# Products of three field pairs from whole tables instead of from the batch's rows, in a pairwise-product recommendation kernel

## What is computed

```python
e = jnp.stack([tbl_0[ids[:, 0]], ..., tbl_39[ids[:, 39]]], axis=1)   # (2048, 40, 64)
viW = jnp.einsum('bpd,pde->bpe', e[:, i_idx, :], W)                  # 780 pairs
z = jnp.einsum('bpe,bpe->bp', viW, e[:, j_idx, :])
h = jnp.concatenate([z, dense_ctx], axis=1)
h = jnp.maximum(h @ W_top1 + b_top1, 0.0)
h = jnp.maximum(h @ W_top2 + b_top2, 0.0)
y = h @ W_top3
```

## Time and profile before

| | us |
|---|---|
| median of 3 runs | 1150.31 (1150.08 to 1150.65) |
| the profiled execution | 1150.38 |
| its span, first to last instruction | 1148.6 |
| PE busy | 1123.7 (98%) |
| DVE busy | 979.0 (85%) |
| ACT busy | 907.7 (79%) |
| POOL busy | 695.8 (61%) |

### The profile page before, as it was taken

The page is one execution under the profiler, slowest core; times in us unless marked ns, Lnnn a source line. Parts: engine busy times, 40 slices in busy tenths (PEclk is TensorE's granted clock), DMA queues, the critical chain, the costliest instruction groups (busy, mean ns, idle before and its releaser), DMA issues.

```text
span 1148.6 us, 46937 instructions
## 1 busy us (share of the span) xinstructions
PE 1123.7 (98%) x17728; PEld 443.4 (39%) x17728; DVE 979.0 (85%) x901; ACT 907.7 (79%) x7245; POOL 695.8 (61%) x837
## 2 busy tenths in 40 slices
PE   6989999999999999999999999999999999999998
PEld 2333333333445333333345433333344533333345
DVE  8599999999866889999975779999986688999960
ACT  1489999998466889999765779999946688999961
POOL 6766655555667667777667767767666766632110
PEclk9999999999999999999999999999999999999999
DMA  6233353232522332333432323333252233222210
GB/s 175 45 95 90 87 152 86 74 92 68 142 54 60 76 88 69 99 89 72 110 103 45 87 71 73 91 89 75 68 144 55 54 82 80 72 80 73 59 32 1
DMA packets 79248, 93.47 MB, mean 81 GB/s; under 512 B 19248, under 2 KB 63040, under 8 KB 78892
## 3 DMA queue, kind: packets, MB, share of 16 engines
q1 hardware_dynamic: 58920, 69.48, 21.2%
q0 software_dynamic: 19456, 19.96, 9.6%
q10 hardware_dynamic: 648, 1.03, 0.3%
HBM read 79.91 MB, written 0.01 MB: 70 GB/s over the span
## 4 chain that ended last, share of the span: by engine, by line
PE 76%; ACT 12%; DVE 7%; issue 4%; DMA 0%; SPq 0%; DVEq 0%
PE Ups L911 29%; PE Ups L904 15%; PE Zps L927 15%; ACT PB L701 11%; PE Ups L956 7%; DVE P L831 4%; PE Ups L889 3%; PE Ups L874 3%; PE Ups L969 3%; DVE PB L819 2%; PE Ups L962 1%; DVE zB L787 1%; DMA V<-tbl 0%; PE Ups L944 0%; ACT V L709 0%
## 5 line engine op out<-in xcount | busy, mean ns | idle before, releaser
L701 ACT ACTIVATE PB<-PB 128x64 f32<-128x64 f32 x3588 | 858.2, 242 | 61.6 <-DVE PB L819 59.4
L701 ACT ACTIVATION_READ_ACCUMULATOR PB<-PB 128x1 f32 x3588 | 674.8, 188 | 0.0
L678 POOL DMA_INDIRECT stage<-tbl,idx x512 | 485.5, 948 | 270.6 <-PE Ups L911 81.9
L831 DVE TENSOR_TENSOR P<-Ups,V 128x1024 f32<-128x1024 f32 x492 | 585.1, 1217 | 45.8 <-PE Ups L911 43.0
L911 PE MATMUL Ups<-V,wf 64*32 64x512 f32 x8192 | 519.1, 591 | 6.8 <-ACT V L709 2.3
L819 DVE TENSOR_TENSOR PB<-Ups,VN 128x1024 f32<-128x1024 f32 (+1 forms) x272 | 327.2, 1203 | 33.6 <-PE Ups L904 30.8
L904 PE MATMUL Ups<-wf,V 64*32 64x512 f32 (+1 forms) x4352 | 287.9, 585 | 4.2 <-DVE P L831 2.4
L927 PE MATMUL Zps<-P,sel 64*32 64x512 f32 x4096 | 273.7, 590 | 0.5 <-DVE P L831 0.5
L911 PEld LDWEIGHTS Ups<-V,wf 64*32 64x32 f32 x8192 | 148.7, 106 | 277.8 <-issue 145.9
L653 POOL TENSOR_TENSOR PB<-PB 128x512 f32<-128x512 f32 (+4 forms) x160 | 97.7, 610 | 78.2 <-DVE PB L819 67.7
L904 PEld LDWEIGHTS Ups<-wf,V 64*32 64x32 f32 x4352 | 78.9, 106 | 147.8 <-issue 96.7
(11 more groups left out here) (40 smaller groups left out, 191.2 us busy)
## 6 DMA issues: line engine op xcount, KB each, us to landing
wf<-w_units SPq DMA_DIRECT2D x336, 160.0 KB
P<-V SPq DMA_DIRECT2D x80, 128.0 KB
stage<-tbl,idx POOLq DMA_INDIRECT x512
w1s<-w SPq DMA_DIRECT2D x1, 1792.0 KB, 7.9
VN<-tbl,idx POOLq DMA_INDIRECT x96
V<-tbl ACTq DMA_DIRECT2D x4, 224.0 KB
V<-tbl SPq DMA_DIRECT2D x4, 224.0 KB
w2s<-w SPq DMA_DIRECT2D x1, 512.0 KB, 8.4
```

Of the source, the lines that this page charges most:

```text
L678: pool.indirect_dma_start(out=natural_rows(m, t)[:, D * f:D * f + D], out_offset=None, in_=tables[field][:, :], in_offset=bass.IndirectOff ...
L701: last = act.activation(p, p, ACT.Copy, accum_out=zB[:, t, at:at + 1])
L831: dve.tensor_tensor(p, Ups[:, slot, :, :rows], v, ALU.mult).then_inc(mul_done, 1)
```

## The change

Pairs k = 11, 7 and 3 (`T_KEYS`) are given fields whose tables have 1000 or 1250 rows (`ORDER` swaps four more fields). For them the product of L904 is not made from the samples' rows: it is made once for all rows of the tables, in 8 + 8 + 10 = 26 steps "tab" of 128 table rows (the same matmul form as a b unit). ACT copies each from `Ups` to SBUF, waits for its own copy, and issues two DMAs that store it to a DRAM scratch `t_rows` (512 columns of U beside 64 of the table; SP copies the table's own rows there with six DMAs). Tabs 0 to 7 lie in the hot phase, two after each "tr"; tabs 8 to 25 lie in group 0, one every 2.6 units from unit 2.2 (`tab_at`). The inputs `t_in` are loaded by SP behind the first hot table, and the third one by ACT behind tab 7.

The gather of those pairs fetches rows of 576 numbers (2304 bytes) instead of 64 into the new tile `UT`, and the 12 b units a group of those pairs become "t" units: no PE step; DVE multiplies `UT` by `VN`; the sums are as before. In groups 1 to 3 a t unit follows every second a unit from the first unit of its key on, and b units follow every 2.10 a units. `V` becomes a ring of 20 pairs and the four for the J fields. The planned pace of gathers after group 0 goes from 1.6, 1.7, 1.8 to 1.55 us, the constants' load waits for the last tab, and `ramp_units` plans down to k = 8.

The core of the diff (left out: renamed tests for "t", the counts `MAINS` that leave t units out of PE's semaphore, and the arrays):

```diff
-for _a, _b in ((31, 35), (23, 36), (21, 39)):
-    ORDER[_a], ORDER[_b] = _b, _a
+T_KEYS, T_VOCAB = (11, 7, 3), (1000, 1000, 1250)
+T_COLS, V_COLS = 2 * JP * D, 2 * JP * D + D
+T_TILES = [-(-_v // P128) for _v in T_VOCAB]
+TABS = [(_i, _x) for _i, _n in enumerate(T_TILES) for _x in range(_n)]
+ROWS = ("b", "t")
+for _a, _b in ((31, 35), (23, 36), (21, 39), (22, 7), (23, 8), (15, 20), (6, 13)):
+    ORDER[_a], ORDER[_b] = ORDER[_b], ORDER[_a]
 HOT_ROWS, HOT_TILES, HOT_CUT = 125, 8, 112
-HOT_IDS, HOT_TABLES = J0, J0 + 2 * JP
+V_RING = 20
+HOT_IDS, HOT_TABLES = V_RING - 2 * JP, V_RING - 4 * JP
...
     here = {k: max(HOT_US, 14.0 + 10.4 * (J0 - k)) for k in range(PAIRS)}
+    b_items, t_items = [u for u in row_units if u[0] == "b"], [u for u in row_units if u[0] == "t"]
     out, a, i, now, act = [], 0, 0, HOT_US, HOT_US
     while a_items[a][1] >= RAMP_TO:
         a_here, b_here = here[a_items[a][1]], here[b_items[i][1]]
-        if b_here <= now and act <= now + DVE_US:
+        if t_items and here[t_items[0][1]] + T_LATER <= now and act <= now + DVE_US:
+            out.append((t_items.pop(0), True))
+            act, now = max(act, now + DVE_US) + ACT_US, now + DVE_US
+        elif b_here <= now and act <= now + DVE_US:
             out.append((b_items[i], True))
             i, act, now = i + 1, max(act, now + DVE_US) + ACT_US, now + DVE_US
...
             i, now = i + 1, now + 2 * DVE_US
         else:
             now = min(a_here, b_here)
-    a0, i0 = a, i
+    a0, i0, due = a, i, 0
     apart = (len(a_items) - A_LAST - a0) / (len(b_items) - i0)
     while a < len(a_items) or i < len(b_items):
-        if i < len(b_items) and a >= a0 + apart * (i - i0) and b_items[i][1] >= a_items[a][1]:
+        if t_items and a >= due and a_items[a][1] < t_items[0][1]:
+            out.append((t_items.pop(0), True))
+            due = a + T_APART
+        elif i < len(b_items) and a >= a0 + apart * (i - i0) and b_items[i][1] >= a_items[a][1]:
             out.append((b_items[i], i % 6 != 5))
             i += 1
         else:
...
-    b_items = [("b", k, t) for k in reversed(range(B_KEYS)) for t in range(TILES[g])]
+    a_items = [item for k in reversed(range(PAIRS)) for item in row_items(k) if item[0] not in ROWS]
+    b_items = [("t" if k in T_KEYS else "b", k, t) for k in reversed(range(B_KEYS)) for t in range(TILES[g])]
     if g == 0:
         return [item for item, _ in ramp_units(a_items, b_items)]
-    out, i = [], 0
+    t_items, b_items = [u for u in b_items if u[0] == "t"], [u for u in b_items if u[0] == "b"]
+    out, i, due = [], 0, 0.0
     for a, item in enumerate(a_items):
         out.append(item)
-        while i < len(b_items) and a >= 2 + 1.74 * i:
+        if t_items and item[1] <= t_items[0][1] and a >= due:
+            out.append(t_items.pop(0))
+            due = a + T_APART
+        while i < len(b_items) and a >= 2 + B_APART * i:
             out.append(b_items[i])
             i += 1
     return out
...
 def v_slot(g, k):
 
 
-    return 2 * J0 + k - J0 if k >= J0 else g % 2 * J0 + k
+    return V_RING + k - J0 if k >= J0 else (J0 * g + J0 - 1 - k) % V_RING
 
 
...
 
 RUN_END, TIES_US, RAMP_UNITS = JP + 4, 40.0, 60
-HOT_STEPS = [("tr", 0, 0)] + [s for _r in range(1, JP) for s in (("tr", 0, _r), ("back", 0, _r - 1))] + [("back", 0, JP - 1)]
+HOT_TABS, TAB_FROM, TAB_APART = 8, 2.2, 2.6
+
+
+def hot_steps():
+
+
+    out, done = [], 0
+    for r in range(JP):
+        out.append(("tr", 0, r))
+        if r:
+            out.append(("back", 0, r - 1))
+        while done * JP < HOT_TABS * (r + 1):
+            out.append(("tab", 0, done))
+            done += 1
+    return out + [("back", 0, JP - 1)]
+
+
+HOT_STEPS = hot_steps()
...
+def tab_at(n):
+
+
+    return TAB_FROM + TAB_APART * (n - HOT_TABS)
...
+def v_before(m):
+
+
+
+    g, r = divmod(m, PAIRS)
+    if r < JP:
+        return J_LAST[g - 1] + 1 if g else 0
+    back = r - JP - V_RING + J0 * g
+    return U0[back // J0 + 1] if back >= 0 else 0
...
+    steps += [(TR_UNIT[n * JP // HOT_TABS] + 0.30004 if n < HOT_TABS else tab_at(n) + 0.00001, ("tab", 0, n))
+              for n in range(len(TABS))]
...
+        def table_in(i):
+
+
+            return w1s[:, :, :].rearrange("p k n -> p (k n)")[:, 1792 * (i % 2):1792 * (i % 2) + 1792]
+
+        def table_out(n):
+
+
+            at = 2 * (n % 2)
+            return h1[:, at:at + 2, :] if n % 4 < 2 else z[:, 2 + at:4 + at, :]
...
+                if r == 0:
+                    for i in range(min(2, len(T_KEYS))):
+                        cols = T_COLS + P128 * T_TILES[i]
+                        sp.dma_start(table_in(i)[:, :cols], t_in[i]).then_inc(tab_loaded[i], 16)
+            for i, k in enumerate(T_KEYS):
+                for f in range(2):
+                    sp.dma_start(t_rows[i][f][:, T_COLS * (1 - f):T_COLS * (1 - f) + D],
+                                 tables[ORDER[2 * k + f]][:, :]).then_inc(rows_stored, 16)
...
                 if c == CONSTS_AT:
+                    sp.wait_ge(tab_done, len(TABS))
...
+                if m == TABLED[0]:
+                    pool.wait_ge(rows_stored, 16 * 2 * len(T_KEYS))
+                if g == 0 and from_table(m):
+                    wait_stored(pool, sum(T_TILES[:T_KEYS.index(PAIRS - 1 - r) + 1]))
                 wait(pool, tr_done, tr_before(m))
                 for t in range(TILES[g]):
+                    if from_table(m) and table_before(m) is not None:
+                        pool.wait_ge(mul_done, pair_units(table_before(m))[t] + 1)
...
+                        if from_table(m):
+                            at = V_COLS * (2 * t + f)
+                            to, rows = UT[:, at:at + V_COLS], t_rows[T_KEYS.index(PAIRS - 1 - r)][f]
+                        else:
+                            to, rows = natural_rows(m, t)[:, D * f:D * f + D], tables[field]
...
+                elif kind == "tab":
+                    i, tile = TABS[x]
+                    slot = U_AT[step] % U_SLOTS
+                    act.wait_ge(tab_done, x + 1)
+                    wait(act, tab_stored[x % 4], 16 * 2 * (x // 4))
+                    act.copy(table_out(x), Ups[:, slot, :, :]).then_inc(tab_copied, 1)
+                    act.wait_ge(tab_copied, x + 1)
+                    ids_here = min(P128, T_VOCAB[i] - P128 * tile)
+                    for f in range(2):
+                        act.dma_start(t_rows[i][f][P128 * tile:P128 * tile + ids_here, D * f:D * f + T_COLS],
+                                      table_out(x)[:ids_here, f, :]).then_inc(tab_stored[x % 4], 16)
+                    if i + 2 < len(T_KEYS) and tile == T_TILES[i] - 1:
+                        cols = T_COLS + P128 * T_TILES[i + 2]
+                        act.dma_start(table_in(i + 2)[:, :cols], t_in[i + 2]).then_inc(tab_loaded[i + 2], 16)
                 elif kind == "z":
+                    if g == 0 and x == 0:
+                        wait_stored(act, len(TABS))
...
+                if unit[0] == "t":
+                    dve.wait_ge(tabled[unit[2]], 16 * 2 * (TABLED.index(g * PAIRS + PAIRS - 1 - k) + 1))
+                else:
+                    slot = U_AT[("main", g, n)] % U_SLOTS
+                    dve.wait_ge(main_done, MAINS[n + 1])
...
+                    at = 2 * V_COLS * unit[2]
+                    u = UT[:, at:at + 2 * T_COLS + 2 * P128].rearrange("p (b c) -> p b c", b=2)[:, :, :cols]
+                    dve.tensor_tensor(PB[:, B_INDEX[n] % PB_SLOTS, :, :cols],
+                                      u if unit[0] == "t" else Ups[:, slot, :, :cols], v, ALU.mult
                                       ).then_inc(mul_done, 1)
...
+                if kind == "main" and UNITS[x][1][0] == "t":
+                    continue
...
+                elif kind == "tab":
+                    i, tile = TABS[x]
+                    pe.wait_ge(tab_loaded[i], 16)
+                    for strip in range(4):
+                        out, at = slice(32 * strip, 32 * strip + 32), T_COLS + P128 * tile + 32 * strip
+                        for f in range(2):
+                            rows = slice(D * f, D * f + D)
+                            last = pe.matmul(Ups[out, slot, f, :], table_in(i)[rows, at:at + 32], table_in(i)[rows, :T_COLS],
+                                             start=True, stop=True)
+                    last.then_inc(tab_done, 1)
```

More of the change, by code:

```diff
@@ L220, in w_layout @@
         item = unit[:2] if unit[0] == "b" else unit
[L221 removed]
+        if unit[0] == "t" or item in place:
             continue
@@ L349, in step_us @@
         return 6.15 if step[2] < 4 else 3.6 if step[2] < 6 else 0.7
+    if step[0] == "main" and UNITS[step[2]][1][0] == "t":
+        return 0.0
     return STEP_US[step[0]]
@@ L362, in schedule @@
     steps += [(mlp_at(g, m), ("mlp", g, m)) for g in range(GROUPS) for m in range(MLP_STEPS)]
+    steps += [(tab_at(n), ("tab", 0, n)) for n in range(HOT_TABS, len(TABS))]
     steps = [s for _, s in sorted(steps, key=lambda x: x[0])]
@@ L368, in schedule @@
```

(21 more changed lines are left out.)

118 lines of the change are left out of this document (74 added, 44 removed).

## The result

The changed kernel takes 1251.58 us (median of 4 runs, 1249.86 to 1256.18) beside 1150.48 for the kernel before (4 runs, 1150.08 to 1150.65): ratio 1.0885, 95% interval 1.0867 to 1.0904. The direction was forecast, the size was not: 101 us instead of 23, far outside 1140 to 1188. The profiled execution is the run of 1256.18, 4.6 above the median.

What follows compares the result with a forecast made beforehand. The prediction took PE, 98% busy, to bound the kernel, with ACT delayed by tabs; hot phase 11, early group 0 28, its rest 0 and groups 1 to 3 -16 gave +23 on 1150.38, so 1173 us, range 1140 to 1188.

Steps and rivals of the forecast that it cites:

- the price of a tab: On ACT, one tab was put at 2.0 us: copy about 0.95, wait 0.1, two DMA issues 1.0.
- Rivals A and B: Tabs on ACT: A, they stay hidden, 1138 us (0.20 with mixtures under 1148); B, issues cost almost nothing, 1155 (0.12).
- The signs for being wrong: ACT has idle time among the tabs, or groups 1 to 3 are not between 263 and 275 us apart.
- Hot phase, +11: Eight tabs before the first unit: 5.2 us of PE plus 6.2 of delay to "back" 3; bounds 7 to 16.
- Six are followed by 7 us of one-hot matmuls, which hide what ACT does: Hot phase: six of its eight tabs cost only PE's time, 5.2 us.
- Group 0 to 102 us, +28: Early group 0: 18 tabs give ACT 36 us, 8 filling its idle time; bounds +20 to +36.
- Group 0 from there, 0 (-8 to +6): Group 0 after 102 us: PE's saving of 7 us gains nothing, as DVE is at 96% with the same work.
- Groups 1 to 3, -16: Later groups: -5.3 us each, PE's -10.3 plus 6.5 lost in bursts less 1.5 between; bounds -9 and +2 a group.
- The credit that I gave each burst, its buffers empty: Groups 1 to 3: three `PB` buffers let ACT lag two units, 7.6 us, so the k = 3 stretch takes 19.
- The ring, SP and POOL at nothing: Costed at nothing: ring of `V`, SP's table copies and longer queue, POOL's gathers; ring about 1 us a group start if late.
- Rival C: On POOL, wide gathers taking twice as long make it the bound, 1206 us; chance 0.08 with other slow cases.
- The product from `UT`: On DVE, taken to cost the same as a product from PSUM, near 1.2 us.

Runs made afterwards that it cites:

- e6: Changed kernel with the tabs' stores and the third input's load issued by SP instead of ACT: 1414.08 us, ratio 1.0718, on a slow chip.
- f9: Changed kernel with the tabs' stores issued by SP, repeated on a third chip; group 0's dense layers begin at 428.65 us, whole time not in the text.
- e3: Changed kernel without its 26 tabs, their inputs, stores and table copies (some products left out, so output differs): 1206.41 us, one run.
- e1: Changed kernel with ACT's copies to `VN` put ahead of the tabs in the hot phase: 1236.11 us, one run.
- e5: Changed kernel with the dense layers' constants loaded three W load slots later: 1426.81 us, ratio 1.0814, on a slow chip.
- e7: Changed kernel with t and b units at one pace in groups 1 to 3, t first: 1426.52 us, ratio 1.0812, on a slow chip.
- f8: Changed kernel with t and b units at one pace in groups 1 to 3, t first, repeated on a third chip: ratio 1.0892.
- e4: Kernel before with only the ring of `V`, the gathers' pace, the order of fields and the constants' later place: 1155.96 us, ratio 1.0047.

## Why the prediction was wrong, by its own steps

- **Direction, and the price of a tab:** right. 1.95 us of ACT against 2.0. Its issues do count: 0.84 us of it, and the 20.7 us of e6 and f9. Rivals A and B fall with them, and e3 shows that tabs were not hidden (50 us). The Trainium skill, "DMA: Bandwidth & Descriptors", gives some 50 ns for a dispatch, in its section on the anatomy of one DMA, which is on DMAs issued by GpSimd. The rows show 0.42 us for each of ACT's issues. The signs for being wrong came: groups 1 and 2 took 283.1 and 289.2 us, outside 263 to 275.
- **Hot phase, +11, measured +24.6.** The step that failed is "Six are followed by 7 us of one-hot matmuls, which hide what ACT does". What follows a pair of tabs on PE is the next table, and its first matmul writes an `Ups` slot that the copy to `VN` must have freed: the dependence I saw for "back" 3 holds for tables 3 and 4 too. The loss is now made up of: four pairs of tabs 7.6, three waits 12.1, and the rest, some 5, matmuls at half clock behind each wait. e1 shows the waits' cause by taking it away. The stop that I did foresee, ahead of "back" 3, was 4.50 us where I had about 4. Nothing in the sum allowed for the clock: in the kernel before it is 1.00 in every window I read, and no stop of PE behind its first matmul is over 1.5 us.
- **Group 0 to 102 us, +28.** e3 gives the tabs 21.2 in all of group 0, inside the bounds of 20 to 36 and near the lower. 18 tabs of 1.95 us are 35, so some 14 us of them fell into time in which ACT had been idle. I had let 8 be filled.
- **Group 0 from there, 0 (-8 to +6), measured +26.** Worst step of the sum beside the next. "DVE is at 96% and its work is the same" was true (234.1 us in the two windows of the earlier trace rows, 234.8 in those of after) and no reason for 0: in a stage where three engines have 4 to 9% to spare, what counts is the order. The row units moved together, nearly all their sums to ACT (9 us and 3.5), a copy got behind the constants (7.6; on its chip e5 shortened these units by 5.2 against e7), and the burst of k = 3 stands there too (7). I costed the place of the constants at nothing: I asked when they are wanted and which W loads stand behind them, not which copies for `P` do.
- **Groups 1 to 3, -16, measured +34.** The step that failed is the size of the bursts, and with it what the stretches between them give back. The 10.3 us of PE that each group saves were to come off in full, with 1.5 more; between the bursts of group 1 they are 5.9. The stretch of k = 3 took 21.6, 21.0 and 23.3 us in the three groups where I had 19. That the dense steps would cover the burst of k = 11 was wrong in group 1, where it cost 4.4, and nearly right in the others. For k = 7 I had 1.1 over PE's own time; against the kernel before it cost 5.8, 12.0 and 6.0. Part of the reason is shown: DVE waits 31.2 us in these groups for `PB` buffers, 0.5 before, and the waits are gone with an even pace (f8). Some stops of PE are followed by half clock, as in k = 7 of group 1; in the burst of k = 3 there the clock stays 1.00. The credit that I gave each burst, its buffers empty, was not the error in group 1: ACT had 3.3 and 3.2 us idle in the ten ahead of k = 7 and k = 3. How the loss divides among waits, clock and dense steps stays open. In time, a run shows the bursts as the cause in group 3 alone, about 7 us.
- **The ring, SP and POOL at nothing.** e4: +5.4 us, of it 2.9 in group 1 and 1.7 in group 2; I had 1 us a group start as its price if late. Which of e4's four parts takes it is open. POOL's first wide gather waited 12.7 us for stored rows where I had 3, but PE waits only 0.2 us for such rows in the whole kernel. SP's table copies held its queue for 17.44 us, so that the loads of W were issued at 29.67 us; e1 starts its first product at 52.24 all the same, so nothing waited for them.
- **Rival C** fell: the wide gathers hold POOL for 946 ns, the 256-byte ones 972.
- **The product from `UT`:** 1237 ns (1.2 was forecast), 20 to 36 longer than one from PSUM (1217 and 1201). The estimate by the Trainium skill's "VectorE: DVE Perf Modes", errata section, had it 65 shorter; the measurement decides, and by it t units cost DVE 1 to 2 us in all.

Open: what of the loss in groups 1 and 2 an even pace of row units gives back on an ordinary chip, and the parts of e4's 5.4 us.

## What to carry to other kernels

When three engines are each above 90% in a stage, don't book the saved work of one before the order of the other two's work is laid out over time: count what each engine owes at the end of a burst, and give new units the even pace that the old ones had. For a step added to an in-order queue, ask for everything behind it in that queue who waits for it, at each place where it is added and not only at the last. A short stop of PE can cost more than its length: here 8.71 and 9.77 us for matmuls of 7.09 behind two stops of 3.8.
